# Edge sum of a graph layer: who multiplies the one-hot matrices of the picked rows by their edge weights

## The reference

```
xn = layernorm(x)
gathered = edge_weight[:, None] * xn[src]
out = segment_sum(gathered, dst, num_segments=6250) + bias
x = x + out + linear_attention(xn)
x = x + experts(layernorm(x))     # top 2 of 8
```

## Time and profile before

| | us |
|---|---|
| median of 3 runs | 2301.28 (2299.09 to 2303.33) |
| profiled execution, time | 2304.95 |
| profiled execution, span | 2302.3 |
| edge sum within the span | about 302 to 1803 |
| granted TensorE clock, mean | 0.968 |

### The profile page before, as it was taken

How to read it: one execution, slowest core, us unless ns; L and a number is a source line. 1 busy time by engine, 2 the same in 40 slices (tenths; PEclk the granted TensorE clock), 3 DMA queues, 4 the chain that set the end, 5 groups by cost and what they waited for, 6 DMA issues and landing times. The chain is left out here.

```text
span 2302.3 us, 45696 instructions
## 1 busy us (share of the span) xinstructions
PE 2107.5 (92%) x16549; PEld 1852.7 (80%) x16550; DVE 2013.1 (87%) x3390; ACT 1129.5 (49%) x1632; POOL 1629.2 (71%) x1364
## 2 busy tenths in 40 slices
PE   7997789999999999999999999999999449999993
PEld 4665678888888888888888888888799439988993
DVE  7998999999999999999999999998788677676662
ACT  2226655555555555555555545553232247666661
POOL 4770067777777777777777777777777347888873
PEclk9997999999999999999999999999999679999996
DMA  4542433333323333333233333332455534444455
GB/s 141 159 115 74 129 120 91 90 100 93 92 88 101 92 91 92 104 91 92 90 102 90 90 99 93 92 92 85 141 155 155 193 68 74 77 76 78 77 76 139
DMA packets 160928, 235.85 MB, mean 102 GB/s; under 512 B 54834, under 2 KB 121805, under 8 KB 160490
## 3 DMA queue, kind: packets, MB, share of 16 engines
q0 software_dynamic: 70896, 164.43, 28.0%
q1 hardware_dynamic: 75536, 55.29, 8.4%
q10 hardware_dynamic: 14314, 13.68, 1.7%
HBM read 186.46 MB, written 53.24 MB: 104 GB/s over the span
## 5 line engine op out<-in xcount | busy, mean ns | idle before, releaser
L815 POOL DMA_INDIRECT picked<-xn_dram,place x1029 | 1182.3, 1149 | 438.0 <-issue 300.1
L913 PE MATMUL bank<-picked,pick_w 128*128 128x256 f32 x2058 | 504.5, 381 | 15.4 <-DMA picked<-xn_dram,place 14.4
L1025 ACT COPY stage<-bank 128x512 f32<-128x512 f32 x343 | 201.0, 586 | 547.7 <-PE bank L901 545.7
L913 PEld LDWEIGHTS bank<-picked,pick_w 128*128 128x128 f32 x2058 | 387.0, 190 | 83.6 <-issue 32.5
L909 PE MATMUL bank<-window,stage 128*128 128x256 f32 x1568 | 382.9, 387 | 0.0
L1286 DVE TENSOR_TENSOR hot_w<-hots,cur 128x1536 bf16<-128x1536 bf16 x343 | 328.6, 958 | 11.9
L979 ACT COPY field_rep<-fields 128x1666 bf16<-128x1666 bf16 (+1 forms) x193 | 322.5, 1675 | 1.2 <-DVE vals L1162 1.2
L909 PEld LDWEIGHTS bank<-window,stage 128*128 128x128 f32 x1568 | 283.8, 191 | 30.7
L1282 DVE TENSOR_TENSOR hots<-ends,cur 128x1408 bf16<-128x1408 bf16 x343 | 302.5, 882 | 1.7 <-ACT cur L1019 1.7
L901 PE MATMUL bank<-hot_w,hots 128*128 128x128 bf16 x4116 | 286.1, 219 | 4.5 <-issue 3.5
L909 PE MATMUL bank<-stage 128*128 128x256 f32 x1176 | 286.0, 386 | 0.0
(11 more groups left out here) (252 smaller groups left out, 3399.5 us busy)
## 6 DMA issues: line engine op xcount, KB each, us to landing
picked<-xn_dram,place POOLq DMA_INDIRECT x1029
xn_dram<-xn ACTq DMA_DIRECT2D x49, 128.0 KB, 1.9
xT_dram<-xT ACTq DMA_DIRECT2D x49, 128.0 KB, 2.1
base_dram<-acc SPq DMA_DIRECT2D x7, 896.0 KB
sum_dram<-acc SPq DMA_DIRECT2D x7, 896.0 KB
z_dram<-vals SPq DMA_DIRECT2D x7, 896.0 KB, 9.8
out_dram<-sum_dram SPq DMA_DIRECT2D x1, 6250.0 KB, 21.7
acc<-in_x_dram SPq DMA_DIRECT2D x6, 896.0 KB, 5.3
```

The costliest lines, as they stand in the source:

```text
L815: pool.indirect_dma_start(out=picked[:, i % SETS * PICK + q, :], out_offset=None, in_=xn_dram, in_offset=bass.IndirectOffsetOnAxis(ap=plac ...
L913: mm = pe.matmul(sum_ps[pp], pick_w[i % SETS][:, q, :], picked[:, i % SETS * PICK + q, :], start=False, stop=(q == PICK - 1))
L1025: act.copy(block_sb[pp].rearrange("p j c -> p (j c)"), banks[pp][:, :]).then_inc(a_copied, 1)
```

## The change

`pick_w` is made by ScalarE in place of VectorE. VectorE's one product a step (128x384, one instruction) goes; ScalarE gets three instructions a step, each a scaled copy of 128x128, whose scale is one value for each partition. The widened weights `cur_w` (one ScalarE copy a unit, L1017) are no longer needed and go too. ScalarE makes `pick_w` of step t+1 right behind `evacuate` of t+1. VectorE's `hots` now also waits for `pick_done`, since ScalarE reads the `hots` buffer that it writes again four steps later.

```diff
@@ tensor
-                pe.wait_ge(pick_done, t + 2)
+                pe.wait_ge(pick_done, t + 1)
@@ scalar, take
-                if half == 0:
-                    act.wait_ge(pick_done, t + 1)
-                    act.copy(cur_w[odd][:, :, :, :].rearrange("p i q r -> p (i q) r"),
-                             weight[par][:, bass.ds(k * BU, BU), :]...broadcast_to([P, BU * PICK, REP]))
@@ scalar
+            def picks(t, i, par):
+                act.wait_ge(hot_done, t + 1)
+                for q in range(PICK):
+                    ins = act.activation(pick_w[i % SETS][:, q, :], hot[i % SETS][:, q, :], ACT.Copy, scale=weight[par][:, t % NT, q:q + 1])
+                ins.then_inc(pick_done, 1)
@@ scalar, unit
                         evacuate(t + i + 1, (odd + i + 1) % 2)
+                        picks(t + i + 1, i + 1, par)
                     elif after:
                         evacuate(t + BU, 1 - odd)
+                        picks(t + BU, 0, 1 - par if turned else par)
@@ vector, hots
                     dve.wait_ge(a_done, free)
+                    dve.wait_ge(pick_done, t - 2)
@@ vector
-            def picks(t, i, odd):
-                dve.wait_ge(hot_done, t + 1)
-                dve.tensor_tensor(pick_w[i % SETS]..., hot[i % SETS][:, 0:PICK, :]..., cur_w[odd][:, i, :, :]..., ALU.mult).then_inc(pick_done, 1)
@@ vector, unit
                 for i in range(BU):
-                    if i + 1 < BU:
-                        picks(t + i + 1, i + 1, odd)
-                    elif after:
-                        picks(t + BU, 0, 1 - odd)
```

More of the change, by code:

```diff
@@ L665, in edge_sum @@
         cur = [sb(f"cur{i}", [P, BU, ROWS, REP], BF16) for i in range(2)]
-        cur_w = [sb(f"cur_w{i}", [P, BU, PICK, REP]) for i in range(2)]
         hot = [sb(f"hots{i}", [P, HOTS, P], BF16) for i in range(SETS)]
@@ L1014, in take @@
                 a, b = ((0, 4), (4, BU))[half]
-                if half == 0:
-                    act.wait_ge(pick_done, t + 1)
-                    act.copy(cur_w[odd][:, :, :, :].rearrange("p i q r -> p (i q) r"),
-                             weight[par][:, bass.ds(k * BU, BU), :].rearrange("p i q -> p (i q)").unsqueeze(2).broadcast_to([P, BU * PICK, REP]))
                 act.copy(cur[odd][:, a:b, :, :].rearrange("p i f r -> p (i f) r"),
                          table[par][:, bass.ds(k * BU + a, b - a), :].rearrange("p i f -> p (i f)").unsqueeze(2).broadcast_to([P, (b - a) * ROWS, REP])).then_inc(cur_done, 1)
+            def picks(t, i, par):
[3 more added lines that the diff above has]
+                ins.then_inc(pick_done, 1)
             def evacuate(t, pp):
@@ L1044, in begin @@
                 take(0, 0, 0, 0, 1)
+                picks(0, 0, 0)
                 evacuate(0, 0)
@@ L1101, in _ @@
             dve.sem_inc(w_done, 1)
-            dve.sem_inc(pick_done, 1)
             dve.tensor_scalar(first_row[:, :], iota[:, 0:NB], float(P), float(-LOWEST), ALU.mult, ALU.add).then_inc(set_up, 1)
@@ L1288, in hots @@
                                   of[:, i, HOTS:ROWS, :].rearrange("p (f g) r -> p f g r", f=PARTS).unsqueeze(3).broadcast_to([P, PARTS, DENSE, RUNS, REP]), ALU.mult).then_inc(w_done, 1)
-            def picks(t, i, odd):
-                dve.wait_ge(hot_done, t + 1)
-                dve.tensor_tensor(pick_w[i % SETS][:, :, :].rearrange("p q (b r) -> p q b r", r=REP),
-                                  hot[i % SETS][:, 0:PICK, :].rearrange("p q (b r) -> p q b r", r=REP),
-                                  cur_w[odd][:, i, :, :].unsqueeze(2).broadcast_to([P, PICK, RUNS, REP]), ALU.mult).then_inc(pick_done, 1)
             def begin():
@@ L1301, in begin @@
                 hots(0, 0, 0, None)
-                picks(0, 0, 0)
                 hots(1, 1, 0, None)
```

## The result

The changed kernel is slower: 2352.18 us (median, 2347.97 to 2352.87) against 2300.91 in the runs made beside it, a ratio of 1.0207 (95% interval 1.0186 to 1.0228). 2355 was forecast, within 2282 to 2392. Its profiled execution took 2347.97 us, with a span of 2346.2, 43.9 above that of before. (The medians are 51.3 apart; the profiled execution of before was a little slower than its median, that of after a little faster.)

What follows compares the result with a forecast made beforehand. GpSimd's gathers were taken to set the pace, 30.45 us a unit against TensorE's floor of 30.01. Longer holding adds 1.31 us over 42 units, +55; 2301.3 + 55 = 2356, rounded to 2355 us, range 2282 to 2392.

Steps and rivals of the forecast that it cites:

- TensorE's floor and the gathers as the pace: Sorting units: TensorE needs at least 30.01 us, but 21 gathers at 1.456 us set the pace, 30.6 against 30.45 measured.
- The rule for a gather's length: A gather lasts 0.95 us plus the rest of the two-input VectorE instruction under which it starts, less about 0.1.
- Removing the product is worth nothing on VectorE: VectorE loses 3.3 us a unit, but TensorE does not wait for it; VectorE will wait at the addition instead.
- The phase term: In sorting steps, gather holding under VectorE's products rises from 0.343 to 0.53 us a step, 1.31 a unit, +55 us.
- The route that the forecast rests on: A gather released at a sorting piece's end has its successor 1.15 us later under `hot_w`: delay 0.54 us, before 0.13.
- the walk of two gathers: Following a released gather and its successor through `hots` and `hot_w`: cost 0.13 us before, 0.54 afterwards, the next one past.
- The signs that were named: Gathers about 1.21 us, most long ones under `hot_w`; units 31 to 32.5; gathered-row waits 60 or more; L1025 never late.
- ScalarE's copies at no cost: ScalarE's 1029 scaled copies, taken as 0.35 us each, fit its idle time and the block copy's 1.9 us to spare.
- The added wait of `hots`: VectorE's `hots` of t+2 waits for ScalarE's `pick_w` of t-1, done more than a step earlier: cost 0.
- The last seven units: End of the edge sum, where VectorE often idles and holds gathers less: no change, 5 us either way.
- The gathers come free: Rival: the product's 28.0 us of blocking goes, units reach TensorE's floor, 2283 us or 2278; chance 0.22.
- ScalarE gets late: Rival: scaled copies over 0.7 us delay `evacuate`, TensorE waits before L909, 2325 to 2345 us; chance 0.03.

Runs made afterwards that it cites:

- e4: Changed kernel plus an unread VectorE sum over 384 columns (one SBUF input) in the old product's place: 2282.15 us, 0.9893 of the kernel before.
- e9: Changed kernel plus an unread VectorE sum over 256 columns in the old product's place: 2279.53 us, 0.9898 of the kernel before.
- e10: Changed kernel without the third gather of each step from the fifth step on, all matmuls kept: 2276.62 us, 0.9883 of the kernel before.
- e1: Changed kernel with ScalarE's scaled copies left out from the fifth step on, so nobody makes new `pick_w`: 2349.78 us, 1.0192 of the kernel before.
- e2: Kernel before plus three unread ScalarE scaled copies of 128x128 a step, VectorE unchanged: 2310.11 us, 1.0011 of the kernel before.
- e3: Changed kernel plus an unread VectorE product of the old shape in the old place: 2310.44 us, 1.0022 of the kernel before.
- e6: Kernel before with VectorE's addition moved from behind `hot_w` to behind the sorting piece in the first 42 units: 2388.73 us, 1.0369 of the kernel before.
- e5: Changed kernel with VectorE's addition moved from behind `hot_w` to behind the sorting piece in the first 42 units: 2317.04 us, 1.0058 of the kernel before.
- e7: Changed kernel with VectorE's addition moved between `hots` and `hot_w` in the first 42 units: 2338.53 us, 1.0147 of the kernel before.

## Why the prediction was right

*TensorE's floor and the gathers as the pace: right.* Units at 30.01 appear in the trace of every kernel whose gathers are fast or few: all 41 units of e4, e9 and e10 take that long, and no sorting unit of any kernel less.

*The rule for a gather's length: right, with one case missing.* It holds in the trace after: 120 gathers that started under nothing took 0.95 on average, 122 under `hot_w` 1.49, 106 under the addition 0.95, and 38 under the sum L1146, one input in SBUF, 0.95 with 0.60 of it left. The last is what e4 was built on. Missing is the gather that starts together with the two-input instruction. In the changed kernel 40 gathers started at most 0.02 us behind the start of `hots` and took 0.95; the next one, 0.055 us behind it, was held. And where the prediction says that whichever issues second blocks, the traces show one direction only: `hot_w` takes 958 ns whether a gather is running when it starts (144 cases) or not (121).

*Removing the product is worth nothing on VectorE: right.* It turned into 145 us of waiting at L1310, 10.8 before in the same window.

*The phase term: right in the sum, not in its parts, and so in part luck.* Forecast were 0.53 us of holding a step under the pair `hots`, `hot_w` in place of 0.34, a mean gather of 1.21 and a unit of 31.8. Measured: 66.4 us under `hot_w` and 58.8 under `hots` in 266 steps, 0.47 a step; the sorting pieces, which I took as unchanged at 73 us in 276 steps (0.26), hold 82 in 266 (0.31). Together +0.17 for the +0.19 forecast, a mean of 1.206 and a unit of 31.65.

The route that the forecast rests on is there, and costs what it says. The successor of a gather that was held under the piece ahead of `hots` starts 1.12 us behind the piece's end: before, under the end of `hots`, for 0.02 us (0.13 was reckoned); after, always under `hot_w`, for 0.54. But it is rare. It occurs in 70 of 275 steps before and in 54 of 265 after, a quarter and a fifth, where the forecast had 54% (three quarters of five in seven). So it brings 28 us, no more than the holding of the removed product takes away. The net growth lies elsewhere: under `hots` 7.2 us became 58.8, 68 of the 106 that were held there behind a gather that was not, while under `hot_w` 59.5 became only 66.4. The agreement with the kernel before (0.35 for 0.34) did not show this, because it too was one of the sum alone. The forecast of 55 us and the 49.0 that 41 units gave are close because errors cancelled. What the experiments show is that the time slot of VectorE's two-input instructions against the gathers makes the slowdown; they do not show that the walk of two gathers gives its size.

*The signs that were named.* The mean gather, the units and VectorE's waits for L912 (218.7 us for 55.6) are as forecast, and TensorE has no wait before L908. Two are not. Of the 405 gathers of over 1.0 us 122 started under `hot_w`, 106 under `hots` and the others under sorting pieces, so most did not start under `hot_w`. And the waits that the profile names after gathered rows came to 50.6 us, not 60 or more, though the weight loads before L912 waited 81.6.

*ScalarE's copies at no cost: right, and shown by e1, e2 and e3.* They take 0.396 us each, 0.99 for three in a row, so 0.30 from start to start; I had taken 0.35. The estimate by the Trainium skill ("ScalarE: Activation LUTs", What ACT_TABLE_LOAD costs: 387 ns with one pointer operand, 93 of overlap, so 0.975 for three) agrees with the trace. The added wait of `hots` cost nothing either: VectorE was idle for 0.0 us ahead of `hots` between 320 and 1520 us.

*The last seven units: "no change, 5 either way" was slightly off.* They are 7.3 us faster. The other traces bear it out: that stretch takes 218.6 to 220.3 us in the four kernels with a product in that place (before, e2, e3, e6) and 208.3 to 217.6 in the others. The start is 3.25 us faster, and the experts' 5.4 the other way lie in the spread of that stretch.

*The rivals.* "The gathers come free" is what e4 and e9 show when the spacer is kept without its holding: 2282 and 2280, the price that was named for it (2283, 2278). The change alone does not get there. "ScalarE gets late" falls with e1, e2 and e10.

## What to carry to other kernels

When GpSimd issues gathers back to back beside VectorE, list VectorE's two-input SBUF instructions as closed doors and the gather's period as a clock, and walk the one through the other, at least one full step on: taking work off VectorE can make the gathers slower, and an idle instruction can make them faster. Trust the walk for where to look, not for the size: it missed that of e5, e6 and e7, and met that of the change in part by luck. A kernel with three engines within 4% of each other answers to such phases more than to loads, so test an order change with an idle spacer of two or three lengths before explaining it. Where one instruction has two waits, don't trust the name the profile gives to the last; take one of the two sources away.

## What the runs showed of the hardware that was not expected

A gather is held only by the VectorE instruction under which it starts, for its rest less about 0.1 us. One that starts a tenth of a microsecond ahead of a `hots` isn't held, and one that starts together with it (up to 0.02 us behind, 40 gathers of the changed kernel) isn't either. The VectorE instruction was not lengthened the other way round: `hot_w` takes 958 ns with and without a gather under way. With the idle sum longer by 0.13 us from start to next start (128 to 256 columns) the whole kernel went from 2362 to 2280 us, 3.5%. That a tensor_reduce of one SBUF input doesn't hold a gather was seen in 38 gathers of the changed kernel and used in e4, where 144 gathers started under the idle sum with a mean length of 0.95.
